# Merging the two halves of a block's probabilities-times-values product, and moving VectorE's copies of turned probabilities ahead of its jobs

## The reference

```python
x = x + tanh(g_xattn[0]) * L0_xattn(layernorm(x), ctx, ctx, ...)   # 16 heads of depth 8, one mask for all
x = x + tanh(g_ffn[0])   * L0_ffn(layernorm(x), weight)            # Hadamard, 4-bit activations, ternary weights
x = x + tanh(g_xattn[1]) * L1_xattn(layernorm(x), ctx, ctx, ...)   # 16 heads of depth 64, masks per batch
x = x + tanh(g_ffn[1])   * L1_ffn(layernorm(x), ...)               # top 4 of 32 experts and a shared one
# attention:
scores = einsum('bhqd,bhkd->bhqk', q, k) / sqrt(D)
attention = softmax(where(mask, scores, low), axis=-1)
out = einsum('bhqk,bhkd->bhqd', attention, v)                      # the "mix" of this text
```

## Time and profile before

| | |
|---|---|
| time, median of 3 runs | 332.14 us (330.86 to 333.17) |
| the profiled execution's own time | 330.76 us, span 328.9 us |
| busy: PE, DVE, ACT, POOL | 292.6, 256.7, 225.6, 117.1 us |
| mix matmuls, L967 | 512 instructions, 52.5 us busy |
| turns, L864 | 512 instructions, 80.2 us busy |
| mask_max, L614 | 128 instructions, 87.5 us busy |
| copies of turned units | VectorE 54 (36.7 us), ScalarE 74 (43.6 us) |
| v on VectorE, L652 | 24 instructions: 16 of 678 ns, 8 of 274 ns |
| transfers | 9.30 MB, nearly all in the first 30 us |

### The profile page before, as it was taken

How to read it: one execution, slowest core, us unless ns; L and a number is a source line. 1 busy time by engine, 2 the same in 40 slices (tenths; PEclk the granted TensorE clock), 3 DMA queues, 4 the chain that set the end, 5 groups by cost and what they waited for, 6 DMA issues and landing times.

```text
span 328.9 us, 6642 instructions
## 1 busy us (share of the span) xinstructions
PE 292.6 (89%) x1963; PEld 211.9 (64%) x1963; DVE 256.7 (78%) x775; ACT 225.6 (69%) x523; POOL 117.1 (36%) x185
## 2 busy tenths in 40 slices
PE   2759899998869798989979999999989989979996
PEld 0546577666546475657646666776757667957995
DVE  1589888788795999999879999999799507566554
ACT  1259698778675989997879998888787532432221
POOL 4346687676463343353123333223323300000000
PEclk9979999999998999999999999999999999999999
DMA  5991000000000000000000000000000000000000
GB/s 162 421 413 53 3 2 2 2 0 4 0 0 2 1 3 0 2 1 2 1 2 1 2 0 2 2 2 1 2 1 1 2 2 0 0 1 18 0 2 16
DMA packets 3603, 9.30 MB, mean 28 GB/s; under 512 B 625, under 2 KB 2289, under 8 KB 3057
## 3 DMA queue, kind: packets, MB, share of 16 engines
q1 hardware_dynamic: 3136, 8.54, 6.6%
q10 hardware_dynamic: 432, 0.35, 0.5%
HBM read 8.62 MB, written 0.26 MB: 27 GB/s over the span
## 4 chain that ended last, share of the span: by engine, by line
PE 51%; DVE 23%; issue 14%; ACT 5%; POOL 3%; DMA 2%; DVEq 0%; ACTq 0%; POOLq 0%
PE bank L864 12%; PE bank L967 11%; DVE masked L614 4%; PE bank L885 4%; PE bank L1009 3%; PE bank L1029 3%; PE bank L889 3%; PE bank L1032 3%; PE bank L942 3%; PE bank L948 2%; PE bank L947 2%; DVE probsT L630 2%; DVE k_both L676 2%; PE bank L882 2%; DMA cols<-in_cols 2%
## 5 line engine op out<-in xcount | busy, mean ns | idle before, releaser
L384 POOL TENSOR_SCALAR probs<-probs,rsum 128x512 f32<-128x512 f32 x128 | 88.9, 697 | 133.6 <-DVE rsum L623 133.1
L450 ACT ACTIVATE probs<-masked,neg_max 128x512 f32<-128x512 f32 x128 | 92.1, 720 | 7.7 <-DVE neg_max L614 6.4
L614 DVE CUSTOM_DVE_ANT_0 masked<-bank,mask 128x512 f32<-128x512 f32 x128 | 87.5, 684 | 7.4 <-PE bank L942 4.9
L864 PE MATMUL bank<-ident,probs 128*128 128x128 f32 x512 | 80.2, 280 | 2.8 <-DVE probsT L630 1.6
L864 PEld LDWEIGHTS bank<-ident,probs 128*128 128x128 f32 x512 | 57.6, 141 | 31.3 <-issue 22.4
L967 PE MATMUL bank<-probsT,val 128*32 128x256 f32 (+1 forms) x512 | 52.5, 396 | 1.8 <-ACT mixT L466 1.7
L458 ACT ACTIVATE probsT<-bank 128x512 f32<-128x512 f32 x74 | 43.6, 590 | 11.9 <-PE bank L864 11.5
L630 DVE COPY probsT<-bank 128x512 f32<-128x512 f32 x54 | 36.7, 679 | 10.2 <-PE bank L864 10.2
L967 PEld LDWEIGHTS bank<-probsT,val 128*32 128x32 f32 (+1 forms) x512 | 22.9, 124 | 27.8 <-issue 16.8
L560 ACT ACTIVATE probsT<-bank 128x256 f32<-128x256 f32 x34 | 13.0, 385 | 36.3 <-PE bank L1029 36.3
L942 PE MATMUL bank<-k,q 128*128 128x512 f32 x64 | 31.7, 501 | 6.2 <-issue 5.9
(11 more groups left out here) (128 smaller groups left out, 449.0 us busy)
## 6 DMA issues: line engine op xcount, KB each, us to landing
we<-in_we SPq DMA_DIRECT2D x3, 1088.0 KB, 14.5
w1T<-in_w1T SPq DMA_DIRECT2D x1, 2048.0 KB, 10.5
w0T<-in_w0T SPq DMA_DIRECT2D x1, 768.0 KB, 7.3
ctxT<-in_ctxT SPq DMA_DIRECT2D x2, 256.0 KB, 5.8
bv<-in_L_xattn_b_V SPq DMA_DIRECT2D x1, 512.0 KB, 10.6
x_sb<-in_x SPq DMA_DIRECT2D x2, 128.0 KB, 5.6
w0T<-in_w0T ACTq DMA_DIRECT2D x1, 256.0 KB, 4.5
m_u<-in_mask SPq DMA_DIRECT2D x1, 256.0 KB, 6.3
```

Of the source, the lines that this page charges most:

```text
L384: pool.tensor_scalar(p, p, rsum[:, u % NCOL:u % NCOL + 1], 1.0, ALU.mult, ALU.mult).then_inc(normed, 1)
L450: act.activation(probs[:, u % NP, :], masked[:, u % NS, :], ACT.Exp, scale=-1.0, bias=neg_max[:, c:c + 1], accum_out=sums[:, c:c + 1]).the ...
L614: dve.tensor_tensor_reduce(out=masked[:, u % NS, :], in0=score_bank[u % 2][:, :], in1=mask, scale=-float(k.depth) ** -0.5, scalar=3.0e38, ...
L864: ins = pe.transpose(dst[0:rows, t * P:t * P + P], src, ident[:, :])
```

## The change

The two entries of `mix_at` become equal, at the step of the second half. TensorE's loop then calls `mix(k, 0)` and `mix(k, 1)` one behind the other in that step. `copy_at` and `out_at` are derived from the second entry and stay. The last block had equal entries already. On VectorE the copy of unit t-1 is issued ahead of the jobs of step t-1 in place of behind them.

```diff
--- before.py
+++ after.py
@@ -76,7 +76,7 @@
         self.end = first + self.units
 
         last = layer == 1 and b == B - 1 and g == self.groups - 1
-        self.mix_at = (self.end + 1, self.end + (1 if last else (2, 3)[layer]))
+        self.mix_at = (self.end + (1 if last else (2, 3)[layer]),) * 2
         self.copy_at = self.mix_at[1] + (2 if layer == 1 and not last else 1)
         self.out_at = self.copy_at + 1
 
@@ -822,10 +822,10 @@
                     mask_max(t + LEAD - 1)
                 if 0 <= t + LEAD - 3 < TOTAL:
                     recip(t + LEAD - 3)
+                if 0 <= t - 1 < TOTAL and not on_act(t - 1):
+                    copy_turned(t - 1)
                 for j in PLAN.get(t - 1, ()):
                     job(j)
-                if 0 <= t - 1 < TOTAL and not on_act(t - 1):
-                    copy_turned(t - 1)
                 if t in (-4, -3, -2):
                     ternary(t + 4)
                 if t == LN01_AT:
```

## The result

The changed kernel takes 334.25 us (median of 15 runs, 332.25 to 337.57), the kernel before, run beside it, 332.82 us (15 runs). The ratio is 1.0053, 95% interval 1.0031 to 1.0074: slower by half a per cent (about 1.8 us), where I had forecast 1.6 us less. Ratios here compare fast runs alone, so this one is not the quotient of the two medians: slow runs such as 338.40 us before and 337.57 us after are left out. The profiled execution took 334.01 us, its span is 332.2.

What follows compares the result with a forecast made beforehand. The prediction took TensorE and VectorE to hold each other in turns. Its terms, 0.87 - 1.15 - 0.3 - 0.1 - 0.95 = -1.6 us with the swap at 0, took 332.14 to about 330.5 us; 0.8 range 325.8 to 334.2.

Steps and rivals of the forecast that it cites:

- The saving per merged pair: TensorE, steady layer 1 block: merging two half mixes saves 0.16 inside, 0.09 at entry, 0.06 behind, about 0.30 us.
- First block: Near 37.5 us: the hole the first half filled stays empty and the whole mix follows it, +0.87 us.
- Next four blocks: Layer 0, TensorE without a gap between the halves: 4 x -0.29 = -1.15 us.
- Sixth block: Near 100 us, in a half-clock stretch: scores go out earlier, the turn behind the mix starts sooner, -0.3 us.
- 104 to 156 us: VectorE holds the pace there, so TensorE's saving buys nothing: 0.
- 156 to 255 us: Gains in free-running blocks, losses where the mix goes behind waits ahead of q: -0.1 us, bounds -2.9 and +1.7.
- Tail: Last blocks: a turn no longer queues behind the 0.62 us wait for ScalarE's mix copy, -0.95 us.
- The swap: VectorE's copies ahead of 19 v jobs: k_both's wait for k_high absorbs added waits, 0 us, bounds -0.4 and +2.6.
- The clock: Half clock entered the sum only through the sixth block, there until about 101.5 us; no term for further stretches.
- Clock as a rival: Empty holes could bring a further half-clock stretch, 1.5 to 1.9 us more, time 337.2 us; chance 0.05.
- rival B: Slower: whole mix behind waits the first half filled, 0.87 us a block, 335.7 us; chance 0.15.
- A: TensorE's saving of 6.9 us survives nearly everywhere: 326.1 us, or 325.5 with the tail's additional 0.6; chance 0.22.

Runs made afterwards that it cites:

- e4: Changed kernel with the first block's mix left in two halves: 332.39 us, ratio 0.9999 to the kernel before.
- e5: Changed kernel, but behind unit 76 alone VectorE does its v job ahead of the copy, as before: 332.96 us, ratio 1.0038 to the kernel before.
- e1: Kernel before with only the mix merged, at the later step; VectorE's copies stay behind the jobs: 333.27 us, ratio 1.0034.
- e7: Kernel before with the mix merged at the later step, copies still behind jobs, plus useless transposes where TensorE waits: 331.16 us, ratio 0.9990.
- e6: Kernel before with useless transposes added where TensorE waits for VectorE, nothing else changed: 331.30 us, ratio 0.9992.
- e9: Kernel before with only VectorE's copies put ahead of its jobs, mix in two halves, plus useless transposes where TensorE waits: 332.67 us, ratio 1.0025.
- late mix: Kernel before with both mix halves at the later step, copies still behind jobs: 333.27 us without fillers (useless transposes), 331.16 us with them.
- e12: Changed kernel with a single filler, 12 useless transposes ahead of the first batch's turned activations: 332.03 us, ratio 1.0010 to the kernel before.
- early mix with fillers: Kernel before with both mix halves at the earlier step, copies still behind jobs, plus useless transposes where TensorE waits: 329.12 us, ratio 0.9920.
- e11: Kernel before with both mix halves at the earlier step, copies still behind jobs, and a larger set of useless transposes: 331.46 us, ratio 0.9978.

## Why the prediction was wrong, step by step

- **The saving per merged pair**, 0.30 us: measured 0.28 in the free-running blocks. Right; each pair has one entry and one exit less. The Trainium skill, "TensorEngine Tiling (Array Packing)", Key Properties, says that a change of tiling mode drains TensorE; the trace agrees with its 0.28 us a pair.
- **First block**, +0.87: measured +0.86 (lag from unit 4's turn to unit 12's), and taken away by e4. Right.
- **Next four blocks**, -1.15: -0.96 (unit 12 to 44's turn, 1.42 to 0.46). Nearly right.
- **Sixth block**, -0.3: **did not hold in the profiled execution**, which has +0.95. I had taken the half-clock stretch as a thing of the place, 3.4 us long; here it was 6.8 us long, and the mix had been moved into it. Where the stretch was 3.4 us the block gave -0.28 (e5, the same code up to there) and -0.36 (e1), and at full clock on both sides (e7 against e6) -0.32. So the sum was right and its premise, one fixed stretch, was not.
- **104 to 156 us**, 0: the lag is 1.41 us at mask_max of unit 57 and 1.40 at unit 80. Right: VectorE holds.
- **156 to 255 us**, -0.1: in the profile, from the turn of unit 56 to that of 120, +2.1, of it 1.47 behind unit 76. Without the swap and with clocks held, e7 moves against e6 by -0.13 us in mask_max from unit 76 to 120, but by +0.37 in the turns from unit 56 to 120. The term itself was about right or up to 0.5 us too low. Its parts came: TensorE's wait ahead of q at 184.71 with the whole mix behind it, and -1.12 for the four free-running blocks.
- **Tail**, -0.95: -0.76. Nearly right.
- **The swap**, 0: **failed**. It costs 1.2 us at one place, between mask_max of units 82 and 84, in two pairs of traces (1.29 less 0.10 for the changed kernel and e5, 1.18 for e9 and e6). I had found the place (the copy at 156.31, v behind it) and the wait on VectorE, 0.8 us; it is 1.00. I let the next wait in VectorE's own queue absorb it, without asking what that wait hangs on. It hangs on ScalarE's k_high, on TensorE's k job, and this one on v: the rotate job just before takes one of the two job banks, so that k gets the bank of v. Delay went around through three engines and came back into the same queue. My list of what is late next had q and the next v, not k. At full clock this step decides the sign: -0.4 us for the late mix, +1.5 with the swap (331.88 against 330.34, few runs). Without fillers it does not do so alone, for the late mix without the swap is at 1.0034 too.
- **The clock**, which the sum had at nothing: **failed**. 0.56 us of the lag come in the start-up and 0.5 among the experts, both with stretches at half clock, beside the sixth block's. Of the median's 1.8 us, one filler takes back 1.4 (e12).
- **Clock as a rival**: rival B named it, with 0.05, as a follow-up of new holes. Its direction held, but not only in the holes: the runs of the changed kernel have mostly a mean clock of 0.979 where the kernel before has 0.984 to 0.990, one or two stretches of 3.4 us more (0.5 x 3.4 / 332 = 0.005 each). The chance was too small.
- **The chances.** The result is within 1%, to which I gave 0.65, but outside my range by 0.05 us and of the other sign. How near it came to the range says little: the changed kernel's own runs differ by more than 3 us. Neither A (the layer 0 and layer 1 blocks held by VectorE gained nothing) nor B's mix mechanism came.

## What to carry to other kernels

A wait that seems to absorb a delay does so only if what it waits for does not depend on the delayed instruction: follow it back through the banks as well as the operands, and look for jobs that shift which bank is whose. Where an engine's clock follows its activity, an edit that removes or bunches its work must be priced with the stretches at either level, and their number belongs to the comparison of runs; timing variants with the waits filled separates that from the edit itself, if the fillers stand ahead of the wait: behind a wait for a bank they cost their full length, here 0.9 and 1.4 us. Merging pieces pays more when the merged piece stands at the earlier place, ahead of the waits that the early piece used to cover: here 2.4 us at full clock (329.94 for the late mix's three runs, 327.54 for the early one's single run), 2.3 by the ratios.

## What the runs showed of the hardware

- The time of one and the same kernel falls into groups by its mean granted clock. Changed kernel: 332.25 us at 0.984 (but 334.13 at 0.985), 333.3 to 334.7 at 0.979, 335.3 and 335.9 at 0.969. Late mix: 331.1 at 0.984, 331.8 to 333.5 at 0.979, 334.6 to 334.9 at 0.969. One stretch more at half clock goes with 0 to 2 us of a 330 us kernel: the early mix with fillers takes 327.54 us at 1.0, 327.61 and 327.72 at 0.995, 328.59 to 330.21 at 0.990.
- 48 useless transposes with their weight loads (the trace has 6732 instructions for 6642) made kernels faster, by 1.5 to 3.0 us in three cases, although 20 of them stood behind waits and cost 2.0 us. "TensorE: Matmul & The Clock Gate" of the Trainium skill (Part 1) says that the array is throttled by default and that activity releases it; the direction agrees. In e11 a larger set of fillers went with a lower mean clock; why is open.
- At half clock TensorE's pieces take nearly twice their place in the queue: the turn at 98.12 us of the changed kernel 0.71 us from its start to the next, the one at 97.45 before 0.35; a half mix 1.87 us for 1.02. The whole mix of layer 0 took 2.77 us with 1.93 of them at half clock: estimated from these, 1.93 / 2 + 0.84 = 1.81 us, near its 1.88 at full clock.
- Two executions of the same instructions up to 100 us, the changed kernel's and e5's, had half clock there for 6.8 and for 3.4 us.
